# Latent attention with a feed-forward layer on eight cores: the context matmuls are issued two panels later, and a head's loads in the fifth panel of the head before

## What is computed

```python
xn = layernorm(x)
q = xn @ Wq + bq;  kv_latent = xn @ Wdown
k = kv_latent @ Wk_up;  v = kv_latent @ Wv_up      # split in heads, RoPE on q and k
scores = einsum('bhqd,bhkd->bhqk', q, k) / sqrt(128)
scores = where(causal, -10000, scores)
ctx = einsum('bhqk,bhkd->bhqd', softmax(scores), v)
x = x + layernorm(ctx @ Wo + bo)
x = x + layernorm(ffn(layernorm(x)))               # silu(gate) * up, int8 weights, inner width 8192
```

## Time and profile before

| | us |
|---|---|
| median of three runs | 8208.26 |
| lowest, highest | 8201.78, 8818.53 |
| profiled execution | 8239.64 |
| its span (first to last instruction), slowest core | 8237.5 |
| spans of the eight cores | 8177.5 to 8237.5 |

### The profile page before, as it was taken

One profiled execution on the slowest core, in us unless ns is written; L12 is line 12 of the kernel. 1 busy time (PEld: TensorE's weight loads), 2 busy tenths in 40 slices (PEclk: granted clock), 3 DMA queues, 4 the chain that ended last, 5 costly groups with the idle time before them and its releaser, 6 DMA issues.

```text
span 8237.5 us, 66762 instructions; the slowest of 8 cores (8177.5 to 8237.5 us)
## 1 busy us (share of the span) xinstructions
PE 4534.4 (55%) x20970; PEld 2137.8 (26%) x21376; DVE 1879.3 (23%) x3445; ACT 1188.5 (14%) x2875; POOL 715.6 (9%) x616
## 2 busy tenths in 40 slices
PE   2334432743333323333333344279989998998997
PEld 0101110321212111111121111134434443443443
DVE  3444543431111111111111123411021112102111
ACT  0000000112222222222222201101000001001100
POOL 1001101320000000000000000011111111111110
PEclk8656665875555555555555567689999999999998
DMA  5322224122333322333333367499789979978985
GB/s 121 86 80 71 72 84 114 47 68 60 64 62 65 73 60 61 61 62 60 64 61 62 72 139 146 109 151 152 158 166 154 158 160 158 152 159 165 153 149 148
DMA packets 1547763, 866.37 MB, mean 105 GB/s; under 512 B 774946, under 2 KB 1522466, under 8 KB 1531682
## 3 DMA queue, kind: packets, MB, share of 16 engines
q0 software_dynamic: 702016, 459.30, 32.8%
q1 hardware_dynamic: 831586, 318.89, 17.2%
q10 hardware_dynamic: 13824, 83.89, 3.1%
HBM read 415.31 MB, written 100.66 MB: 63 GB/s over the span
## 4 chain that ended last, share of the span: by engine, by line
PE 45%; DMA 23%; DVE 10%; ACT 9%; issue 7%; POOL 3%; SPq 2%; another core or an unknown queue 1%; ACTq 0%; DVEq 0%; POOLq 0%
DMA arena<-arena 15%; PE ps L953 11%; PE ps L967 10%; PE ps L1017 10%; ACT arena L683 7%; PE ps L719 6%; DMA ctxr<-xin 3%; PE ps L794 2%; PE ps L655 2%; POOL arena L448 2%; PE ps L409 2%; PE ps L378 2%; DVE smalls L677 1%; POOL arena L573 1%; DMA ctxr<-x_scr 1%
## 5 line engine op out<-in xcount | busy, mean ns | idle before, releaser
L719 PE MATMUL ps<-arena 128*128 128x128 bf16 x4352 | 503.8, 309 | 1824.2 <-DMA arena<-arena 1824.2
L953 PE MATMUL ps<-ctxr,arena 128*128 128x512 bf16 x4013 | 929.3, 382 | 238.7 <-DMA ctxr<-x1n_scr 123.3
L683 ACT ACTIVATE arena<-ps,smalls 128x512 bf16<-128x512 f32 (+1 forms) x1152 | 747.5, 666 | 2157.6 <-PE ps L655 1282.7
L719 PEld LDWEIGHTS ps<-arena 128*128 128x128 bf16 x4352 | 443.6, 144 | 1943.5 <-issue 1943.5
L967 PE MATMUL ps<-ctxr,arena 128*128 128x512 bf16 x4015 | 920.1, 379 | 4.3
L1017 PE MATMUL ps<-arena 128*128 128x512 bf16 x4014 | 881.7, 379 | 15.1 <-DVE arena L988 6.9
L953 PEld LDWEIGHTS ps<-ctxr,arena 128*128 128x128 bf16 x4096 | 402.9, 98 | 725.6 <-issue 249.0
L655 PE MATMUL ps<-arena 128*128 128x512 bf16 (+1 forms) x1064 | 459.4, 525 | 218.5 <-ACT arena L683 168.2
L1017 PEld LDWEIGHTS ps<-arena 128*128 128x128 bf16 x4096 | 399.7, 98 | 497.1 <-issue 17.7
L967 PEld LDWEIGHTS ps<-ctxr,arena 128*128 128x128 bf16 x4096 | 400.7, 98 | 483.3
L983 DVE TENSOR_SCALAR arena<-ps,smalls 128x512 bf16<-128x512 f32 x256 | 192.2, 751 | 1453.0 <-PE ps L967 1452.7
(11 more groups left out here) (74 smaller groups left out, 2607.2 us busy)
## 6 DMA issues: line engine op xcount, KB each, us to landing
arena<-wg POOLq DMA_DIRECT2D x128, 1024.0 KB, 6.7
arena<-wu POOLq DMA_DIRECT2D x128, 1024.0 KB, 7.3
arena<-wd POOLq DMA_DIRECT2D x128, 1024.0 KB, 5.5
ctxr<-xin SPq DMA_DIRECT2D x32, 1024.0 KB, 5.9
arena<-wo POOLq DMA_DIRECT2D x16, 2048.0 KB, 15.7
xnf_scr<-arena SPq DMA_DIRECT2D x16, 1024.0 KB, 7.1
k_scr<-ctxr SPq DMA_DIRECT2D x16, 1024.0 KB, 7.1
v_scr<-ctxr SPq DMA_DIRECT2D x16, 1024.0 KB, 7.9
```

Of the source, the lines that this page charges most:

```text
L683: s.activation(P_b[par][:, n0:n0 + N], psa[:, 0:N], ACT.Exp, bias=negc[:, par:par + 1], scale=1.0, accum_out=lacc[:, par * 8 + ci: par * 8 ...
L719: r = t.matmul(cpa[:, 0:128], PT_b[par][:, kc, :], v_t[hp][:, kc, :], start=(kc == 0), stop=(kc == W // 128 - 1))
L953: rr = t.matmul(ga, wg_s[slp][:, fc, icw * 128:(icw + 1) * 128], x1nfm[:, fc, :], start=(fc == 0), stop=(fc == NH - 1))
```

## The change

The loads of a head become a function `head_loads`. It is called for head 0 ahead of the loop, and for head h+1 in panel tt = 4 of head h, ahead of that panel's steps. The context matmuls and the scaling become a function `emit_ctx`. A panel no longer issues them for itself: it is put into the list `pend`, and when that holds more than two panels, the oldest is issued. So the context of panel p-2 is written behind the scores, exps, sums and the transpose of panel p, on PE and on DVE, across the heads too. What is left at the end is issued ahead of the barrier. The context's bank (4 or 5) is picked by another count. Buffers, shapes and the number of instructions stay.

```diff
--- before.py
+++ after.py
@@ -619,8 +619,7 @@
 
         s_m.produced(st("Q", lambda q: q.dma_start(mks_s, mks), dma="dQ"))
 
-        pancnt = 0
-        for h in range(NH):
+        def head_loads(h):
             hp = h % 2
             ev = st("S", lambda s, h=h, hp=hp: s.dma_start(
                 k_s[hp], k_scr[h * 128:(h + 1) * 128, :]),
@@ -638,11 +637,47 @@
                 dma="dA")
             s_q[hp].produced(ev)
 
+        head_loads(0)
+        pend = []
+
+        def emit_ctx(p):
+            (par, hp, W, tt, h) = p
+            cbank = 4 + (len(pend) + h + tt) % 2
+            cps, cpa = ps_slot[cbank], ps_ap[cbank]
+
+            def fn(t, par=par, hp=hp, W=W, cpa=cpa):
+                r = None
+                for kc in range(W // 128):
+                    r = t.matmul(cpa[:, 0:128], PT_b[par][:, kc, :],
+                                 v_t[hp][:, kc, :],
+                                 start=(kc == 0), stop=(kc == W // 128 - 1))
+                return r
+            ev_c = st("T", fn, waits=prod_waits(cps) +
+                      cons_waits(s_PT[par], s_v[hp]))
+            cps.produced(ev_c)
+            s_PT[par].used(ev_c)
+            s_v[hp].used(ev_c)
+
+            ev_e = st("V", lambda v, tt=tt, h=h, par=par, cpa=cpa:
+                      v.tensor_scalar(ctx[:, tt, h * 128:(h + 1) * 128],
+                                      cpa[:, 0:128],
+                                      rl_s[:, par:par + 1], None,
+                                      op0=ALU.mult),
+                      waits=cons_waits(cps, s_rl[par]))
+            cps.used(ev_e)
+            s_rl[par].used(ev_e)
+            s_ctx.produced(ev_e)
+
+        pancnt = 0
+        for h in range(NH):
+            hp = h % 2
+
             for tt in range(16):
+                if tt == 4 and h + 1 < NH:
+                    head_loads(h + 1)
                 par = pancnt % 3
                 pancnt += 1
                 W = wpad(tt)
-                nch = (W + 511) // 512
                 nch = (W + 511) // 512
                 exp_evs = []
                 ev_nc = None
@@ -710,31 +745,12 @@
                 s_P[par].used(ev_t)
                 s_PT[par].produced(ev_t)
 
-                cbank = 4 + (pancnt % 2)
-                cps, cpa = ps_slot[cbank], ps_ap[cbank]
-
-                def fn(t, par=par, hp=hp, W=W, cpa=cpa):
-                    r = None
-                    for kc in range(W // 128):
-                        r = t.matmul(cpa[:, 0:128], PT_b[par][:, kc, :],
-                                     v_t[hp][:, kc, :],
-                                     start=(kc == 0), stop=(kc == W // 128 - 1))
-                    return r
-                ev_c = st("T", fn, waits=prod_waits(cps) +
-                          cons_waits(s_PT[par], s_v[hp]))
-                cps.produced(ev_c)
-                s_PT[par].used(ev_c)
-                s_v[hp].used(ev_c)
-
-                ev_e = st("V", lambda v, tt=tt, h=h, par=par, cpa=cpa:
-                          v.tensor_scalar(ctx[:, tt, h * 128:(h + 1) * 128],
-                                          cpa[:, 0:128],
-                                          rl_s[:, par:par + 1], None,
-                                          op0=ALU.mult),
-                          waits=cons_waits(cps, s_rl[par]))
-                cps.used(ev_e)
-                s_rl[par].used(ev_e)
-                s_ctx.produced(ev_e)
+                pend.append((par, hp, W, tt, h))
+                if len(pend) > 2:
+                    emit_ctx(pend.pop(0))
+
+        while pend:
+            emit_ctx(pend.pop(0))
 
         plan.barrier()
```

## The result

The changed kernel is faster: it takes 0.8074 of the time of the kernel before, 95% interval [0.8055, 0.8094]. The profiled execution took 6630.2 us, of which 6628.7 us are its span. Before it was 8239.6. The forecast was 6682, range 6560 to 6900.

What follows compares the result with a forecast made beforehand. Serial order of exp, transpose, context and scores bounds the attention stage. 16 x (79.0 + 1.7) + 15 x (3.5 + 4.0) = 1404, with the end 1413 instead of 2939 us; profiled 6714, median 6682, range 6560 to 6900.

Steps and rivals of the forecast that it cites:

- The ring through the transpose: In each attention panel, exp, transpose of P, context and scores ran one after another; 184 us a head with its tail.
- DVE string: Between panels: sum, reciprocal, scaling, maximum; from the sum to the next exp 1.78 us per panel.
- boundary: Between heads: contexts of panels 14 and 15 and transpose(15) delay the next head's first exps; +3.5 us, 15 times.
- The rival that the change does nothing: Context(p-2) waits as long as context(p) did, needing a panel 15 transpose of over 13 us; same time: chance 0.01.
- the slower one: Attention transposes 2.4 times as slow or more make the kernel slower than before; 8400 us at 2.6 times; chance 0.02.
- free-running head: One head's exps plus the small DVE instructions between panels, without waits for transposes: 79.0 us, 16 times.
- context late in wide panels: Panels 12 to 15: scores wait for banks, so context and scaling come late and delay the next exp; +1.7 us per head.
- moved loads: At the fifth panel: V's issue holds SP, so the transpose of panel 4 lands late; +4.0 us, 15 times.
- the rival of slower transposes: Attention transposes slower when overlapped with exps and matmuls: 6842 us at 1.25 times, 7130 at 1.5; chance 0.15.
- The clock rival: PE's clock rises with its density, shortening contexts in wide panels and between heads: 51 us in all, 6631; chance 0.30.
- The other figure for transposes: The skill page's estimate for panel 15's transpose, 2.8 us instead of 6.66: total 34 us lower, about 6648; not used.

Runs made afterwards that it cites:

- e7: The changed kernel with every transpose of P cut to its first 256 keys, output not right: attention stage 1249 us, 87 less.
- e5_six_banks: The changed kernel with the scores spread over six PSUM banks instead of four: attention stage 1321 us, 15 less.
- e9: The changed kernel with V's transpose in four pieces, issued in panels 4, 6, 8 and 10: attention stage 1310 us, 25 less.
- three edits: The changed kernel with next panel's first maximum ahead of the sum, six score banks and context three panels late: attention stage 965 us.

## Why the prediction was right

**The mechanism** held in its main steps. The ring through the transpose was the bound. Two panels of distance take it away, and what remains is exps plus a DVE string, with the boundary and the loads on top. I had said that I would be wrong if ACT waited for scores instead of the maximum. Of ACT's idle before the exps, 353 us are released by the maximum and 181 by the scores; these are the panels behind the loads and those that wait for a bank, and the rest of the panels go by the maximum. The rival that the change does nothing, and the slower one, fell with the result. e7 and the unchanged 1.61 us speak against engines slowed by transfers.

**The sizes**, in us a head, for the head above (84.9 against 88.2 forecast) and for all heads of the same core. The last column is the difference to the forecast over the stage, from all heads:

| term | forecast | head above | all heads | over the stage |
|---|---|---|---|---|
| free-running head | 79.0 | 74.8 | 75.2 | -60 |
| context late in wide panels | 1.7 | 1.9 | 1.3 | -6 |
| boundary | 3.5 | 5.9 | 5.0 | +23 |
| moved loads | 4.0 | 2.3 | 2.5 | -22 |

The last three are ACT's idle above the floor of 1.61 in panels 8 to 15, in panel 2, and in panels 6 and 7; the free-running head is what is left. Terms of a head count 16 times, boundary and loads 15 times. They add up to -65, and the stage from first to last exp came out 65 below my sum. On the other cores the last three are 1.3 to 1.5, 4.9 to 5.3 and 2.4 to 2.7. That the total is this near owes something to luck: boundary and loads were each wrong by a third or more, and their errors cancel.

*Free-running head.* The term that was mis-sized is the DVE string, which I had put together from neighbours of before. The changed kernel's own timeline in a panel without waits reads:

```profile
2286.33 0.15 DVE L730 TENSOR_REDUCE smalls<-smalls 128x1 f32<-128x2 f32 x1 [1.41 <-ACT arena L718]
...
2286.59 0.16 DVE L734 RECIPROCAL smalls<-smalls 128x1 f32<-128x1 f32 x1
2286.69 0.35 DVE L662 TENSOR_SCALAR ctxr<-ps,smalls 128x128 bf16<-128x128 f32 x1
...
2286.96 0.68 DVE L712 TENSOR_REDUCE smalls<-ps 128x1 f32<-128x512 f32 x1
...
2287.84 0.69 ACT L718 ACTIVATE arena<-ps,smalls 128x512 bf16<-128x512 f32 x1 [1.61 <-DVE smalls L712]
```

Sum to reciprocal is 0.26 as forecast. But the scaling starts 0.10 after the reciprocal, not 0.26. I had taken the sum and the reciprocal as the model for this pair, and there the second needs the result of the first. The scaling of context(p-2) doesn't need the reciprocal of panel p: its own one is two panels old. So it starts before the reciprocal, shown as 0.16 long, has ended. The maximum follows the scaling by 0.27, not 0.36: in the row of before it had the scores to wait for, which PE began only at 3198.93, behind the context. The exp follows the maximum by 0.88. The string is 1.51 instead of 1.78 us, 256 times, 69 us; the whole term came out 60 lower.

*Wide panels.* The forecast made the context late there because scores 4 and up wait for a bank. `e5_six_banks` bears that out: with six banks these waits are gone. 0.5 of the 1.3 us are in panels 9 and 10, for which I had reckoned nothing.

*Boundary.* Two things made it longer. The transpose of panel 15 took 7.56 us instead of 6.66, as the chain has it:

```profile
2269.23 7.56 DMA arena<-arena
...
2276.93 3.58 PE ps L651 x32
```

Landing later, it held up context 15, which cost its full 3.6 us at the low clock. And with the shorter string, and context 14 at the upper clock, the panels beside it had become shorter, so that there was less to hide it behind. The transfers' median from issue to landing rose from 4.4 to 4.9 us over the stage. So the rival of slower transposes was right in sign, by 11% in the median. What slows them is open: e7 shortened them and can't tell.

*Moved loads.* V did hold SP's line, for 6.95 us; e7 bears out that the waits of panels 6 and 7 are the loads', and e9 that panel 7's is V's hold on SP. It was 2.3 us in this head instead of 4.0 because the transpose of panel 4 went out on SP 8.6 us after the sum of panel 3 (2286.33 to 2294.92), where I had taken 9.5 to 12.6, and I had then chosen the upper part of the range of 1.8 to 4.9.

*The clock rival* had two parts. The clock did rise, from 0.57 to 0.70 over the stage, with PE busy 836 of 1353 us instead of 929 of 2943. By the rule of the Trainium skill that the prediction cites (TensorE: Matmul & The Clock Gate, Part 1) activity releases the throttle, and the trace agrees. The terms that it was to remove partly stayed: context 14 fell to 1.84 us as reckoned, and context 15 did not, because the wait in front of it lets the clock fall. Its 6631 was nearer to the time than my sum was, but the 51 us between the two are less than what the free-running term alone was off (60 us), and that was the DVE string. That rival had the right time mostly for another reason.

*The other figure for transposes* (the Trainium skill, Advanced Engine Details and Errata, X-Bar Transpose (TRN2): 350 to 400 GB/s expected) was not borne out. The row after (7.56 us for 1.05 MB, 139 GB/s) is further from it than the one before, and e7 shows that the time is on the path.

## What to carry to other kernels

Where the chain is a ring through every engine and none is half busy, write the consumer of a slow transfer some iterations later in the program, and count the iterations by the widest transfer against the *narrowest* iterations that follow it: here one panel of distance left the ring in place, two were enough except where wide panels meet narrow ones, and the third gave 99 us. What remains then is the string of small instructions between the last and the next large one; read its pitches from start to start, and for each pair ask whether the second needs the first, since an error of 0.27 us counts 256 times. Waits that lie over one another hide each other: three edits worth 247 us alone gave 370 together, until the DMA engines and SP had hardly a pause left.

## What the hardware showed unexpectedly

- Two small DVE instructions on one engine, the second waiting for the first, started 0.26 us apart (sum, reciprocal). The scaling, which needs neither of them, started 0.10 us behind the reciprocal although that is shown as 0.16 long. In the same timeline a maximum shown as 0.68 long is followed by a mask that doesn't need it after 0.60 (2286.96 to 2287.56), and a mask shown as 0.42 long by the maximum over its result after 0.53 (2269.79 to 2270.32).
- Behind an idle PE of 4.89 us between two groups of matmuls the granted clock had fallen from the upper level to the lower: 0.061 and 0.11 us for the same matmul. Behind ten more matmuls and 1.93 us it had not. Matmuls without a reader, in a wait that exists anyway, gave 23 us.
- The transpose of panel 15 took 6.66 us with the compute engines idle, in the last head of the kernel before, and 7.56 us beside other work, 8.07 in the last head of the changed kernel. Its issue on SP rose too, from 4.86 to 5.52 us.
- V's transpose in four pieces gave 25 us with the DMA engines' share at 0.71. With the share at 1.00, and SP issuing for all but 35 of 950 us, it gave nothing; the 25 us that it cost there were seen in one execution only.
